# Moving batch 1's query, key and value projections out of the last expert passes and in among the first score maxima (one core)

## The reference, cut to what matters

```
x = hidden_states                                   # 4 batches x 1024 tokens x 128
x = x + 0.5 * experts(layernorm(x))                 # 8 experts, each takes its 256 best tokens of a batch
x = x + attention(layernorm(x))                     # 16 heads of 8, rotary angles, softmax over 1024 keys
x = x + 0.5 * experts(layernorm(x))
```

## Time and profile before

| what | us |
|---|---|
| median of 3 runs (lowest to highest) | 1216.72 (1214.67 to 1217.55) |
| the profiled execution | 1206.15 |
| its span, first to last instruction | 1204.2 |
| PE busy in the span | 1080.4 |
| DVE busy | 978.6 |
| ACT busy | 769.9 |
| POOL busy | 592.7 |

### The profile page before, as it was taken

One profiled execution on the slowest core, in us unless ns is written; L12 is line 12 of the kernel. 1 busy time (PEld: TensorE's weight loads), 2 busy tenths in 40 slices (PEclk: granted clock), 3 DMA queues, 4 the chain that ended last, 5 costly groups with the idle time before them and its releaser, 6 DMA issues. The chain is left out here.

```text
span 1204.2 us, 25196 instructions
## 1 busy us (share of the span) xinstructions
PE 1080.4 (90%) x9412; PEld 472.4 (39%) x9412; DVE 978.6 (81%) x1938; ACT 769.9 (64%) x1461; POOL 592.7 (49%) x615
## 2 busy tenths in 40 slices
PE   6199899899499999999999999999998889899993
PEld 6066566565141222222222222222222256466753
DVE  5766966575979999999999999999997675876641
ACT  3063232532368999999989999899999835222220
POOL 4046788765468611100013357455520177678886
PEclk7589999999598999999999999999999988999997
DMA  8024456448614220212111122111310135345543
GB/s 268 31 82 94 90 115 136 82 114 193 151 37 123 58 62 22 60 43 61 36 30 43 43 61 54 30 43 43 96 45 7 26 97 123 81 90 107 111 101 29
DMA packets 93072, 93.84 MB, mean 78 GB/s; under 512 B 14684, under 2 KB 70236, under 8 KB 92920
## 3 DMA queue, kind: packets, MB, share of 16 engines
q1 hardware_dynamic: 70424, 75.46, 22.3%
q0 software_dynamic: 22528, 16.79, 10.0%
HBM read 64.02 MB, written 30.13 MB: 78 GB/s over the span
## 5 line engine op out<-in xcount | busy, mean ns | idle before, releaser
L1828 DVE TENSOR_REDUCE mx<-pA 128x2 f32<-128x1024 f32 x512 | 585.3, 1218 | 13.7 <-PE pA L1380 13.0
L1132 ACT ACTIVATE Pt<-pS 128x512 f32<-128x512 f32 x1024 | 556.3, 596 | 29.7 <-PE pS L1465 24.0
L1444 PE MATMUL pO<-Pt,Vst 128*16 128x256 f32 x4096 | 321.0, 385 | 12.8 <-ACT U L1123 12.8
L1027 ACT ACTIVATE Pt<-pS 128x512 f32<-128x512 f32 x128 | 76.4, 597 | 199.4 <-PE pS L1294 199.2
L622 POOL DMA_INDIRECT xg<-zd,idx x128 | 126.0, 985 | 156.4 <-DVE idx L1635 86.3
L1380 PE MATMUL pA<-Kst,Qst 48*128 48x512 bf16 x704 | 140.9, 397 | 20.1 <-DVE mx L1828 18.9
L1444 PEld LDWEIGHTS pO<-Pt,Vst 128*16 128x16 f32 x4096 | 68.0, 94 | 204.4 <-issue 106.3
L1465 PE MATMUL pS<-Qst,Kst 51*128 51x512 bf16 x704 | 138.5, 390 | 3.7 <-ACT Pt L1132 0.7
L1294 PE MATMUL pS<-Pt,wg 128*128 128x512 f32 x256 | 137.6, 620 | 4.1 <-DVE Pt L1662 2.0
L702 POOL TENSOR_TENSOR mparts<-mx,onesm 128x32 bf16<-128x32 f32 x16 | 4.0, 252 | 269.3 <-DVE mx L1833 213.0
L1305 PEld LDWEIGHTS pA<-wd,Pt 128*128 128x128 f32 x960 | 114.5, 193 | 17.1 <-issue 16.3
(11 more groups left out here) (223 smaller groups left out, 1188.4 us busy)
## 6 DMA issues: line engine op xcount, KB each, us to landing
wg<-w_gate_dram SPq DMA_DIRECT2D x32, 256.0 KB
wu<-w_up_dram SPq DMA_DIRECT2D x32, 256.0 KB
wd<-w_down_dram SPq DMA_DIRECT2D x32, 256.0 KB
qk<-parts SPq DMA_DIRECT2D x64, 96.0 KB, 2.4
Kst<-qk SPq DMA_DIRECT2D x132, 32.0 KB
zd<-Z SPq DMA_DIRECT2D x8, 512.0 KB, 3.8
vp<-pair SPq DMA_DIRECT2D x4, 1024.0 KB, 4.6
Vst<-vp SPq DMA_DIRECT2D x16, 256.0 KB
```

The costliest lines, as they stand in the source:

```text
L1132: S.activation(Pt[:, s % 4, j, r * 512:(r + 1) * 512], pS[:, bank_of(k, 4 * s + 2 * j + r), :], ACT.Exp, scale=SCALE).then_inc(s_exp, 1)
L1444: last = M.matmul(pO[32 * h:32 * h + 16, cols], Vst[k][:, s % 8, h, :], Pt[:, s % 4, h // 2, (h % 2) * 512 + 256 * a:(h % 2) * 512 + 256 * ...
L1828: V.reduce_max(mx2[:, k, 2 * j:2 * j + 2, c, half], pA[ring[q, a] % 2][:, :, :], AX.X).then_inc(s_Ar, 1)
```

## The change

- Units 2 and 3 (batch 1, ten products) leave passes 14 and 15 and become window uses after pieces 0, 2, 4, 6 (unit 2) and 8, 10, 12, 13 (unit 3), in the form that units 4 to 7 have: out of PSUM by ScalarE, multiplied and added by GpSimd.
- ScalarE: `middle(2)`, `high(3)`, `middle(3)` move in between the roots, the normalisation and the transpositions of batches 2 and 3. GpSimd: six products and sums come after `scatter(15)`, with `rest` and `lowest` between them.
- SyncE: `store_values(0)` goes behind `load_weights(15)`; `store_values(1)` goes behind the loads of weights 16 and 17 and of batches 2 and 3.
- The down weights get a semaphore of their own, `s_wd`, on which `down` and `last_down` wait; `gate_up` waits for two transfers instead of three.
- `veps` goes; a tile `eps` is filled by GpSimd at the start, and the root adds it as ScalarE's bias.

```
@@ tables
-    for m in range(5, 25):
+    for m in range(5, 15):
         place[divmod(55 + m, 5)] = ("s", m)
...
-    for u, at in ((4, 22), (5, 28), (6, 32), (7, 37)):
-        for i in range(4):
-            window[divmod(at + i, 32)] = ("PR", u, i)
+    for u, ats in ((2, (0, 2, 4, 6)), (3, (8, 10, 12, 13)), (4, range(22, 26)), (5, range(28, 32)), (6, range(32, 36)), (7, range(37, 41))):
+        for i, at in enumerate(ats):
+            window[divmod(at, 32)] = ("PR", u, i)
@@ sync
-                sp.dma_start(wd[p]...).then_inc(s_w[p], 16)
+                sp.dma_start(wd[p]...).then_inc(s_wd[p], 16)
...
-            store_values(0)
             store_parts(0)
             load_weights(15)
+            store_values(0)
             store_parts(1)
             load(0)
             load(1)
-            store_values(1)
             load_weights(16)
             load_weights(17)
             for b in range(2, B):
                 sp.wait_ge(s_scat[b], 256)
                 load_x(b, x1_in)
+            store_values(1)
@@ gpsimd
+            GP.memset(eps[:, :], EPS).then_inc(s_fill, 1)
...
             scatter(RUN - 1)
+            product(2, 0)
+            product(2, 1)
+            add_products(2)
+            product(3, 0)
             rest(2)
+            product(3, 1)
+            add_products(3)
+            lowest(2)
             rest(3)
-            lowest(2)
             lowest(3)
@@ scalar
-                S.activation(sd[:, tiles(i)], veps[:, tiles(i)], ACT.Sqrt).then_inc(s_sd, 1)
+                S.activation(sd[:, tiles(i)], mv[:, tiles(i), 1], ACT.Sqrt, bias=eps[:, 0:1]).then_inc(s_sd, 1)
...
-            middle(2)
-            middle(3)
...
+            for u in (2, 3):
+                for i in range(4):
+                    projected(u, i)
+                value_rows(u)
+            high(2)
             deviation(6)
+            middle(2)
             deviation(7)
             act.wait_ge(s_sd, 8)
             S.activation(warm[:, :], sd[:, 0:8], ACT.Exp)
             normalise(6)
+            high(3)
             turned_half(0)
             turned_half(1)
+            middle(3)
             normalise(7)
@@ tensor
-                    pe.wait_ge(s_w[p], 48 * (it // 2 + 1))
+                    pe.wait_ge(s_w[p], 32 * (it // 2 + 1))
...
+                    pe.wait_ge(s_wd[p], 16 * (j // 2 + 1))
...
-                pe.wait_ge(*was_read(("s", 24) if j < RUN else ("f", 3, NF - 1)))
+                pe.wait_ge(*was_read(("s", 14) if j < RUN else ("f", 3, NF - 1)))
@@ vector (moments)
-                link(last)
-                V.tensor_scalar(veps[:, tiles(i)], mv[:, tiles(i), 1], EPS, None, ALU.add).then_inc(s_ve, 1)
+                last.then_inc(s_ve, 1)
```

More of the change, by code:

```diff
@@ L113, in program @@
         stats = sb("stats", [P, CH, 6], F32)
-        veps = sb("veps", [P, T], F32)
+        eps = sb("eps", [P, 1], F32)
         sd = sb("sd", [P, T], F32)
@@ L215, in program @@
         room = onehot[:, :, :, :].rearrange("p b c s -> p (b c s)").bitcast(F32).rearrange("p (i n) -> p i n", i=2)
-        pairs = {4: (scr[:, 0, :], scr[:, 2, :]), 5: (scr[:, 1, :], scr[:, 3, :]), 6: (room[:, 0, :], room[:, 1, :]),
-                 7: (U[1][:, :], U[2][:, :])}
+        pairs = {u: (scr[:, u % 2, :], scr[:, 2 + u % 2, :]) for u in range(2, 6)}
+        pairs |= {6: (room[:, 0, :], room[:, 1, :]),
+                  7: (U[1][:, :], U[2][:, :])}
         dens = sb("dens", [P, P], F32)
@@ L276, in program @@
         s_w = [sem(f"w{i}") for i in range(2)]
+        s_wd = [sem(f"wd{i}") for i in range(2)]
         s_xtr = sem("xtr")
@@ L394, in load_weights @@
                     sp.wait_ge(s_down, j - 1)
-                sp.dma_start(wd[p][:, :, :], t["w_down"][e].rearrange("(i p) d -> p i d", p=P)).then_inc(s_w[p], 16)
+                sp.dma_start(wd[p][:, :, :], t["w_down"][e].rearrange("(i p) d -> p i d", p=P)).then_inc(s_wd[p], 16)
             def store_z(i):
@@ L435, in store_values @@
             def store_values(b):
-                if b < 2:
-                    sp.wait_ge(*was_read(("s", 10 * b + 14)))
+                if b == 0:
+                    sp.wait_ge(*was_read(("s", 14)))
                 else:
-                    sp.wait_ge(s_vs, 2 * b - 2)
+                    sp.wait_ge(s_vs, 2 * b)
                 sp.dma_start(vp[b * G:(b + 1) * G].rearrange("g p f -> p g f"),
@@ L695, in add_products @@
                 a, b = pairs[u]
-                pool.wait_ge(s_mul, 2 * (u - 3))
+                pool.wait_ge(s_mul, 2 * (u - 1))
                 GP.tensor_tensor(a, a, b, ALU.add).then_inc(s_roped, 1)
@@ L799, in affinities @@
                 last.then_inc(s_affc, 1)
-            pool.wait_ge(s_fill, 2)
+            pool.wait_ge(s_fill, 3)
             gains(0)
@@ L906, in deviation @@
                 act.wait_ge(s_ve, nth(i))
-                S.activation(sd[:, tiles(i)], veps[:, tiles(i)], ACT.Sqrt).then_inc(s_sd, 1)
+                if i == 0:
+                    act.wait_ge(s_fill, 3)
+                S.activation(sd[:, tiles(i)], mv[:, tiles(i), 1], ACT.Sqrt, bias=eps[:, 0:1]).then_inc(s_sd, 1)
             def normalise(i, first=0, end=CH):
@@ L1077, in value_rows @@
             def value_rows(u):
-                act.wait_ge(s_v, u - 3)
+                act.wait_ge(s_v, u - 1)
                 values_out(u, pO[:, :]).then_inc(s_vs, 1)
+            for u in (2, 3):
[3 more added lines that the diff above has]
+            high(2)
             deviation(6)
+            middle(2)
             deviation(7)
@@ L1352, in warm_up @@
                     M.matmul(pY[:, 0:P], ones[:, :], ones[:, :], start=True, stop=True)
-            pe.wait_ge(s_fill, 2)
+            pe.wait_ge(s_fill, 3)
             warm_up(24)
@@ L1404, in window_use @@
                     if i == 0:
-                        pe.wait_ge(s_winr, win["T", 2 * (b - 2) + 1] + 1)
-                    last = project(op, (wq, wr)[i // 2], 2 * (b - 2) + i % 2, bank)
+                        pe.wait_ge(*(was_read(("s", 4)) if b == 1 else (s_winr, win["T", 2 * (b - 2) + 1] + 1)))
+                    last = project(op, (wq, wr)[i // 2], 2 * (b % 2) + i % 2, bank)
                 else:
@@ L1412, in window_use @@
                     u = key[1]
-                    if u > 4:
-                        pe.wait_ge(s_vs, u - 4)
+                    if u > 2:
+                        pe.wait_ge(s_vs, u - 2)
                     project_values(u, pO[:, :]).then_inc(s_v, 1)
@@ L1421, in _ @@
             pe.wait_ge(s_ye, RUN)
-            pe.wait_ge(*was_read(("s", 24)))
+            pe.wait_ge(*was_read(("s", 14)))
             pe.nop().then_inc(s_mt, 1)
@@ L1432, in _ @@
             pe.wait_ge(s_winr, len(win))
-            pe.wait_ge(s_vs, 4)
+            pe.wait_ge(s_vs, 6)
             pe.nop().then_inc(s_pv, 4)
@@ L1521, in moments @@
                 ts = range(i % B * CH, (i % B + 1) * CH)
+                if i:
+                    dve.wait_ge(s_ve, nth(i) - 1)
                 for n in ts:
@@ L1814, in _ @@
             last.then_inc(s_zlo, 1)
-            dve.wait_ge(s_fill, 2)
+            dve.wait_ge(s_fill, 3)
             for n in range(NF):
```

## The result

The median of the kernel after is 1208.58 us (1202.76 to 1213.30), of the kernel before in the same runs 1216.70 (1214.67 to 1220.01): so 8.1 us less. The ratio is 0.9926, 95% interval 0.9908 to 0.9943. A ratio is estimated here from all runs of both kernels and is not the quotient of the two medians; this one stands for 9.0 us (7 to 11). The forecast was 1208.2 and a gain of 8.5. The profiled execution took 1207.84 us, its span 1206.0. That is *more* than the 1206.15 of before's profile. Before's was an exceptional execution, under all of its eleven timed runs, so the two totals are not compared; stages are.

A forecast was written before the change was run, and what follows sets the result against it. PE was taken to bound passes 14 and 15, and DVE the pieces after. 9.74 - 0.5 - 1.3 - 0.2 - 0.2 + 0.5 + 0.5 = 8.5 us, so 1216.72 becomes 1208.2 (range 1205.0 to 1210.5, widened to 1204.8 to 1213.5).

The forecast's parts named there:

- Part 1: Passes 14 and 15 lose ten products and the wait before `last_down`: 9.74 us gained at most, 7 at least.
- Part 2: Load of group 0 ahead of the first piece, behind unit 1's stored parts: costs 0.5 us (0.1 to 3).
- Part 3: The window of pieces takes the ten products at PE's full clock: costs 1.3 us (0 to 14.8).
- Part 4: ScalarE and GpSimd inside the window: `deviation(6)` and `deviation(7)` come in time; costs 0.2 us (0 to 0.7).
- Part 5: Reload of batches 2 and 3, which waits for `scatter(15)`: costs 0.2 us (0 to 0.9).
- Part 6: Own semaphore `s_wd` shortens PE's wait before the first product of pass 2: gains 0.5 us (0 to 1.4).
- Part 7: Nine `veps` instructions go from VectorE; nothing gained at the start by the skill's rule: gains 0.5 us (0 to 1.4).
- A: Rival: transfers or GpSimd take over around the load, window and reload; 2 to 4 us less gain, 1211; chance 0.17.
- B: Rival: clock falls in the window, every second piece free of a projection; 7.0 instead of 1.3 us, 1213.9; chance 0.12.
- C: Rival: clock 1.2 GHz from the first piece, nothing covered; 14.8 instead of 1.3 us, 1221.7; chance 0.06.
- D: Rival: passes shrink, but a wait that was met early takes it all back; 1216.7; chance 0.07.

The follow-up runs named there:

- the run in rows: The kernel with the split waits, its eight projections placed behind consecutive pieces (0 to 3 and 10 to 13) instead of mostly every second one: 1209.13 us, ratio 0.9929.
- the two small edits: The kernel before with only the constant as ScalarE's bias (`veps` gone) and the down weights' own semaphore: 1214.68 us, ratio 0.9971.
- the split waits: The kernel after, with only those transfers of the first group's load that need unit 1's stored rows waiting for them: 1207.55 us, ratio 0.9906.
- the move alone: The kernel after with both small edits taken back, so moved products and reordered transfers only: 1218.19 us, ratio 1.0001 of the kernel before.

## Why the prediction was right, term by term

The forecast hit the time (1208.2 against 1208.58), and the direction and the main mechanism are shown. But it hit by terms whose errors partly cancel and by 2.0 us that no stage explains, and so far it was luck. One of its own signs of being wrong came near: counted from pass 14 as in the kernel before, the first piece stands at 291.9 (foreseen 290 to 290.5, wrong later than 292), released by a transfer.

**Part 1, 9.74 us: right.** The two passes and the gap ahead of `last_down`: from VectorE's first multiplication of pass 14 to `last_down` 28.76 us before, 18.88 after, 9.88 less. With the load out of the way, 34.11 - 24.15 = 9.96. PE has no gap in either pass, so the lower bound of 7 did not come true.

**Part 2, 0.5 us: mis-sized.** Between 26.34 or 25.59 and 24.15: 2.2 and 1.4 us, within the bounds of 0.1 and 3. The step that failed is the choice between two rows: I took the issues of unit 1's parts nearer to 3.89 than to 6.81 us since "the value store is two us ahead of the parts". They took 5.02, and with 5.02 the same chain gives 1.3 us. The rest of the first profile's 2.2 is the landing: from the last issue of the load to the first piece 4.2 us, where 3.2 had been counted (3.4 in the second profile). Moving the value store 6.6 us forward brought 3.77. By the rule quoted from the Trainium skill ("DMA: Bandwidth & Descriptors", "Issuing engines are not separate DMA queues") the upper end should have been paid. The runs bear it out in kind (5.02 against 3.77 us), and lie between the ends.

**Part 3, 1.3 us: right at the full clock, which didn't come from the start.** At the full clock the twelve pieces cost 14.42 - 13.58 = 0.84 us. Unit 2's value product holds VectorE up for 0.50 us there, the last bracket of the rows of pieces above, and not for the 1.04 of the earlier trace rows, where the piece ahead of it had a projection too. After measured 1.77 and 2.72 more than before. The failing step is "up to the first piece PE is full": it forgot what a late load does to the clock. With 3.29 us of idle PE ahead of the first piece the clock was 0.59 in the first 3.4 us. In the four profiles with 1.11 or 1.29 us and the alternating placement it stayed 1.00 up to piece 12; in the six with 2.33 us or more it didn't. That the alternating placement holds the clock was right, and the run in rows shows its worth: 2.9 us, 1.9 of them from piece 7 on, where the clock had fallen.

**Part 4, 0.2 us: the wrong wait.** `deviation(6)` and `deviation(7)` came in time, as worked out. The margins were spent otherwise: GpSimd, moved forward by the change, now works beside VectorE's two shifts, and these take 0.97 and 1.15 us instead of 0.17, and piece 14 to piece 20 is 1.77 us longer. Holding GpSimd back undoes all of it. The Trainium skill ("SBUF — State Buffer", "Who interferes with whom") says that a DVE instruction with two SBUF inputs contends with a GpSimd instruction that reads SBUF, and calls the shared ports an exclusive lock. The common ends in the two timelines agree. I had looked at that section for the start alone, and not asked which VectorE instructions GpSimd would now stand beside.

**Part 5, 0.2 us: nothing.** The reload was issued at 302.14, and VectorE went from piece 12 to the moments without a gap.

**Part 6, 0.5 us: 0.7.** The wait in pass 2 was 1.42, 1.38, 1.30 and 1.60 us in the four profiles with the shared semaphore, and between 0.33 and 1.00 in the ten without; the means are 1.43 and 0.70. In the times it can't be told once `veps` is gone.

**Part 7, 0.5 us: much too small, and here terms don't add.** Without the move the two small edits bring 3.5 us (1.6 to 5.6), against 1.0 in the sum. With the move the constant alone is worth about 4 (1209.89 against 1213.93): its addition for unit 7 takes 1.98 us beside GpSimd when it is there, a third victim. Part of the rest shows as a later first piece in both profiles with `veps` (28.00 and 27.71 against 25.59 to 26.95 in three without), with the clock that this costs. Why the load should be later with `veps` in, or whether these two executions were only unlucky, stays open, and so does why the semaphore is worth 5 us with `veps` and nothing without. At the start nothing was gained: the first writes of Z begin at 7.33 us before and at 6.77 after, and end at 10.6 in both, 0.15 us after GpSimd's last fill (10.45 and 10.48). This agrees with the rule of the Trainium skill ("SBUF — State Buffer", "Who interferes with whom") that the prediction's part 7 used.

```profile
6.77 3.86 DVE L1827 TENSOR_SCALAR Z<-X,mv,rstd 128x128 f32<-128x128 f32 x4
```

**The sum as measured** (first profiles): 10.0 of passes, less 2.2 for the load, 1.8 for clock and value product and 1.8 for the shifts, plus 0.4 (`veps`, twice) and 0.9 between piece 20 and the exponential, is 5.5 us; with the 0.6 of pass 2, 6.1. The 2.0 us that are missing to the 8.1 of the medians (2.9 to the 9.0 of the ratio) lie outside these stages, where profiles of one kernel differ by 5 us; the small edits have a remainder of 1.4 there. I can't assign it.

The range's bounds don't follow from the terms as the prediction says: parts 1, 6 and 7 whole are 9.74 + 1.4 + 1.4 = 12.5 us and not 11.7, and with part 1 at 7 the gain is 5.8 and not 6.2.

**The rivals.** A came true in its first part and not in the others: the load was late; GpSimd was not, but it cost 1.8 us in a way that A didn't have. B and C, the clock: neither held at its price; a part of B's price (0.9 to 1.9 of 5.7 us) was paid, for another reason than B's. D did not happen.

## What to carry to other kernels

When work is taken out of a stretch that binds, look up what was hidden behind that work, and mend its chain of store, wait and load in the same change: here either of two edits of SyncE's order brought the load in time and the clock with it (in one of the three profiles that had only the split waits for it, the load was late all the same). Ask of every engine that starts earlier what it will stand beside: a 0.17 us instruction on VectorE can cost what the GpSimd operation next to it costs. And test parts of a change together as well as apart: the small edits alone gave 3.5 us, the move alone nothing, both together 9.0 and 9.4 by the same kind of ratio.

## What the runs showed of the hardware

- Two kinds of small VectorE instructions on 128 x 8 elements waited for a GpSimd operation on 128 x 1024: 0.80 to 1.98 us instead of 0.17, ending 0.02 to 0.03 us after it, in every profile that had them side by side. They are a two-input one (shift) and a one-input addition of a constant (`veps`). The maxima out of PSUM, the moments and the reciprocals beside the same operations kept their 1.2, 1.6 and 0.19 us.
- PE's clock after an idle stretch in the middle of full work: 1.11 and 1.29 us of idleness left it at 1.00, after 3.29 us it was 0.59 in the next 3.4 us, and after 2.33, 4.45 and 4.93 us the first projection took 2.07 us instead of 1.12. After 3.01 us the first one still took 1.13 and the second 2.07: the length of the pause alone doesn't set the moment.
- The same eight store issues (unit 1's) took 3.7 to 4.1 us in the six profiles without the value store close ahead of them, and 4.9 to 5.5 us in the eight with it 1.9 us ahead. Right behind the value store, 0.4 us, unit 0's eight took 6.3 to 6.9 us.
